# Routed experts of a Perceiver block on sorted tokens: eight expert products of full width become eight passes over nine slots of half-width expert pairs

## What is computed

```python
flat = x.reshape(S, C)                                   # S = 1024 tokens, C = 512
shared = _swiglu(flat @ W_shared_in) @ W_shared_out      # hidden width HID = 1024
g_idx = jnp.argmax(softmax(flat @ Wg_gate + group_bias), -1)      # one of G = 2 groups
in_group = e_group[None, :] == g_idx[:, None]            # 4 of the 8 experts
p_expert = softmax(where(in_group, e_logits, -inf)) * g_prob
topv, topi = jax.lax.top_k(p_expert, 2)                  # w: 2 of 8 weights not zero
h = _swiglu(flat @ W1_shared)
routed = sum over e of  h @ W2_experts[e] * w[:, e:e + 1]
out = _rmsnorm(x + shared + routed, norm2_w)             # and the block adds its input
```

## Time and profile before

| | us |
|---|---|
| median of 3 runs (3694.50 to 3694.57) | 3694.51 |
| profiled execution, its own time | 3685.18 |
| span of that execution | 3683.4 |
| TensorE busy in the span | 3438.0 (93%) |
| dense stage, first matmul at | 3091.47 |
| experts, first matmul at | 3318.20 |

### The profile page before, as it was taken

The page is one execution under the profiler, slowest core; times in us unless marked ns, Lnnn a source line. Parts: engine busy times, 40 slices in busy tenths (PEclk is TensorE's granted clock), DMA queues, the critical chain, the costliest instruction groups (busy, mean ns, idle before and its releaser), DMA issues. The chain is left out here.

```text
span 3683.4 us, 51408 instructions
## 1 busy us (share of the span) xinstructions
PE 3438.0 (93%) x18898; PEld 2918.1 (79%) x18898; DVE 1869.9 (51%) x3079; ACT 1477.5 (40%) x2740; POOL 1583.6 (43%) x1072
## 2 busy tenths in 40 slices
PE   6999999999999999999999978899895867999998
PEld 4888888888888888888888857678774655787886
DVE  3455555455555555554555565665665374221115
ACT  3455555555555555555555421533542142120000
POOL 4455555455545545554555440422431351433440
PEclk9999999999999999999999988999997988999999
DMA  5111111011111101110111041000002101111111
GB/s 206 58 44 42 37 34 43 35 44 44 42 37 44 44 29 39 44 44 35 44 44 36 3 144 35 26 26 1 3 1 89 32 1 43 58 46 46 46 46 40
DMA packets 103901, 161.40 MB, mean 44 GB/s; under 512 B 10192, under 2 KB 70736, under 8 KB 94928
## 3 DMA queue, kind: packets, MB, share of 16 engines
q1 hardware_dynamic: 103632, 158.02, 13.1%
HBM read 139.12 MB, written 18.87 MB: 43 GB/s over the span
## 5 line engine op out<-in xcount | busy, mean ns | idle before, releaser
L427 POOL TENSOR_TENSOR es<-es,e 128x512 f32<-128x512 f32 x480 | 622.2, 1296 | 966.4 <-ACT e L493 966.1
L489 ACT ACTIVATE e_hl<-sc 128x512 fp32r<-128x512 f32 x512 | 323.8, 632 | 738.8 <-DVE sc L557 738.5
L585 PE MATMUL ps_p<-c_hi,wkv_lo 128*128 128x512 f32 x1024 | 402.7, 393 | 4.6 <-PEq L115 4.6
L585 PE MATMUL ps_p<-c_lo,wkv_hi 128*128 128x512 f32 x1024 | 402.4, 393 | 0.0
L585 PE MATMUL ps_p<-wkv_lo,c_hi 128*128 128x512 f32 x1024 | 401.6, 392 | 0.0
L585 PE MATMUL ps_p<-wkv_hi,c_lo 128*128 128x512 f32 x1024 | 401.5, 392 | 0.0
L585 PE MATMUL ps_p<-c_hi,wkv_hi 128*128 128x512 f32 x1024 | 399.3, 390 | 0.0
L515 DVE TENSOR_TENSOR k_lo<-ps_p,k_hi 128x512 fp32r<-128x512 f32 x256 | 175.9, 687 | 440.0 <-ACT k_hi L455 440.0
L585 PE MATMUL ps_p<-wkv_hi,c_hi 128*128 128x512 f32 x1024 | 398.3, 389 | 0.0
L515 DVE TENSOR_TENSOR v_hl<-ps_p,v_hl 128x512 fp32r<-128x512 f32 x256 | 177.3, 692 | 428.1 <-ACT v_hl L455 427.1
L557 DVE TENSOR_SCALAR sc<-ps_s,topi 128x512 f32<-128x512 f32 x512 | 379.9, 742 | 0.3 <-PE ps_s L635 0.2
(11 more groups left out here) (351 smaller groups left out, 7111.1 us busy)
## 6 DMA issues: line engine op xcount, KB each, us to landing
raw<-in_ctx_t SPq DMA_DIRECT2D x64, 1024.0 KB, 4.8
dense_raw<-in_L_ffn_W_experts SPq DMA_DIRECT2D x32, 512.0 KB, 3.6
raw<-in_L_xattn_Wkv SPq DMA_DIRECT2D x4, 1024.0 KB, 4.9
q_hi_scratch<-qa_qh SPq DMA_DIRECT2D x16, 256.0 KB, 2.5
q_lo_scratch<-qa_ql SPq DMA_DIRECT2D x16, 256.0 KB, 3.4
q_hi<-q_hi_scratch SPq DMA_DIRECT2D x32, 128.0 KB, 5.0
q_lo<-q_lo_scratch SPq DMA_DIRECT2D x32, 128.0 KB, 4.7
o_t_scratch<-o_sb SPq DMA_DIRECT2D x32, 128.0 KB, 2.3
```

The lines of the kernel that those rows point to most:

```text
L427: g.tensor_tensor(ES[:, GL], ES[:, GL], e, ALU.add).then_inc(summed, 1)
L489: a.activation(E2[:, s % 2, :, 0, :], sc, ACT.Exp, scale=DH ** -0.5).then_inc(exp_hi, 1)
L585: mm = t.matmul(ps_p[:, par % 2, :], lhs, rhs, start=m == 0, stop=m == 3 * KC - 1)
```

## The change

What it does, in the dense stage:

- Tokens are sorted by group. TensorE counts ranks with 9 small matmuls (`rank`), VectorE makes each token's new place (`place`) and, for each block of 128 sorted tokens, a register value that says which group its first token is of (`steer`, `REGS`). GpSimd scatters rows to three DRAM buffers with indirect DMAs: 8 of the weights and the token's number (`ms_d`), 8 of the rows (`xs_d`), and, after the shared expert, 8 of the sums (`bs_d`).
- The shared expert still runs on the tokens in their old order. Between its output blocks TensorE transposes the sorted rows (`XS`, 8 x 4 transposes), and the second branch runs on sorted tokens.
- The experts: a pass `u` of 8 takes experts p and 4 + p, and of both the same 256 of the 512 output columns (`UNITS`). A block of sorted tokens needs the one half or the other of the 512 columns in SBUF. TensorE loads the block's register (`value_load`) and the 24 matmuls take 256 moving columns from the address made of it. The block in which the groups meet is done twice, for group 0 and (slot `B`, from a copy `HB_hi`, `HB_lo`) for group 1: nine slots in a pass.
- The weights come in the same 4 pieces of 128 x 1,024 for each pass, now as two DMAs of runs of 256 columns.
- The norm is taken after the last slot, four blocks together; GpSimd adds the input rows (8 indirect gathers after the second group of experts) and scatters the result to `out` (8 indirect DMAs).
- Loops over experts are written out.

The diff, cut to the parts that the text speaks of:

```diff
+        HB_hi, HB_lo = (flat(XT_lo[:])[:, n * HK * P:(n + 1) * HK * P].rearrange("p (k f) -> p k f", k=HK) for n in range(2))
...
+        XS = SG
+        X2 = flat(XT_hi[:]).bitcast(F32).rearrange("p (b f) -> p b f", b=B)
+        OUT = ROWS
...
+        NS = B + 1
+        SLOTS = (0, 1, 2, 3, B, 4, 5, 6, 7)
+        UNITS = [(p, o) for p in range(EPG) for o in range(2)]
...
+            def expert_group(u):
+                p, o = UNITS[u]
+                for q in range(GP):
+                    sp.wait_ge(w_lo_done, GP * (u + 4) + q + 1)
+                    dst = RAW[:, q].rearrange("p (k g f) -> p k g f", k=2, g=GROUPS_E)
+                    for g in range(GROUPS_E):
+                        src = w2[EPG * g + p].rearrange("(k p) n -> p k n", p=P)
+                        sp.dma_start(dst[:, :, g, :], src[:, 2 * q:2 * q + 2, o * EH:(o + 1) * EH]).then_inc(raw_in[q], 16)
+
+            def load_sorted(j):
+                sp.dma_start(XS[:, j % 2], xs_d[j * P:(j + 1) * P]).then_inc(xs_in[j % 2], 16)
+            sp.dma_start(ORDER[:], order).then_inc(order_in, 16)
...
+            sp.wait_ge(meta_sent, 16 * B)
+            sp.dma_start(META_S[:], ms_d.rearrange("(b p) f -> p b f", p=P)).then_inc(meta_in, 16)
+            sp.wait_ge(x_sent, 16 * B)
+            sp.wait_ge(h_done, TH * HK)
+            load_sorted(0)
+            load_sorted(1)
+            for j in range(2, B):
+                sp.wait_ge(xs_turned, j - 1)
+                load_sorted(j)
             hidden_group(w1, 3, 0)
+            sp.wait_ge(base_sent, 16 * B)
+            sp.dma_start(ROWS[:], bs_d.rearrange("(b p) f -> p b f", p=P)).then_inc(base_in, 16)
             hidden_group(w1, 4, GP)
-            with sp.Fori(0, E_ALL) as e:
-                out_group(w2[bass.ds(e, 1)].rearrange("o k n -> (o k) n"), e + 5)
-            for b in range(B):
-                sp.wait_ge(final, b + 1)
-                sp.dma_start(out[b], OUT[:, b % 2]).then_inc(stored[b % 2], 16)
-                if b + 2 < B:
-                    sp.dma_start(X2[:, b % 2], x2_d[b + 2]).then_inc(x2_in[b % 2], 16)
-            for par in range(2):
-                sp.wait_ge(stored[par], 16 * B // 2)
+            for u in range(len(UNITS)):
+                expert_group(u)
...
+            def scatter(dst, src, b, sent):
+                g.indirect_dma_start(dst, bass.IndirectOffsetOnAxis(ap=POS[:, b:b + 1], axis=0), src, None).then_inc(sent, 16)
+            g.wait_ge(placed, 1)
+            g.wait_ge(meta_set, 2)
+            for b in range(B):
+                scatter(ms_d, META[:, b], b, meta_sent)
+                scatter(xs_d, ROWS[:, b], b, x_sent)
...
+            g.wait_ge(xs_in[1], 16 * (B // 2))
+            for b in range(B):
+                g.wait_ge(added, b + 1)
+                scatter(bs_d, ROWS[:, b], b, base_sent)
+            split(4, A_)
+            for u in range(len(UNITS)):
+                split(5 + u, (B_, A_)[u % 2])
+                if u == 1:
+                    g.wait_ge(ids_set, 1)
+                    for j in range(B):
+                        g.indirect_dma_start(X2[:, j], None, x2_d.rearrange("b p f -> (b p) f"),
+                                             bass.IndirectOffsetOnAxis(ap=IDS[:, j:j + 1], axis=0)).then_inc(x2_in, 16)
+            g.wait_ge(x2_in, 16 * B)
+            for j in range(B):
+                g.wait_ge(scaled, j + 1)
+                g.tensor_tensor(OUT[:, j], ROWS[:, j], X2[:, j], ALU.add).then_inc(final, 1)
+                g.wait_ge(final, j + 1)
+                g.indirect_dma_start(out.rearrange("b p f -> (b p) f"), bass.IndirectOffsetOnAxis(ap=IDS[:, j:j + 1], axis=0), OUT[:, j], None
+                                     ).then_inc(stored, 16)
+            g.wait_ge(stored, 16 * B)
...
+            a.wait_ge(steered, 1)
+            edge = a.value_load(REGS[0:1, B:B + 1], min_val=0, max_val=B - 1)
+            a.wait_ge(h_hi, 2 * TH * HK)
+            a.copy(HB_hi.rearrange("p k (o f) -> p k o f", o=1), HT_hi[:].rearrange("p k (t f) -> p k t f", f=P)[:, :, bass.ds(edge, 1), :]
+                   ).then_inc(hb_done, 1)
...
+                rank = bank(4)[:, 0:B]
+                link(v.tensor_scalar(N0[:], bank(4)[:, B:B + 1], -1.0, float(TOK), ALU.mult, ALU.add))
+                link(v.tensor_tensor(PA[:], TOKEN, rank, ALU.subtract))
+                link(v.tensor_tensor(PB[:], rank, PA[:], ALU.subtract))
+                link(v.scalar_tensor_tensor(out=PB[:], in0=PB[:], scalar=N0[:], in1=SEL[:, 0, :], op0=ALU.add, op1=ALU.mult))
+                link(v.tensor_tensor(PA[:], PA[:], PB[:], ALU.add))
+                v.tensor_copy(POS[:], PA[:]).then_inc(placed, 1)
...
+                link(v.tensor_scalar(SIDE[:], EDGE, N0[:], None, ALU.is_ge))
+                link(v.tensor_tensor(EDGES[:], SIDE[:, 1:], SIDE[:, 0:B], ALU.subtract))
+                link(v.tensor_copy(REGS[:, 0:B], SIDE[:, 0:B]))
+                link(v.tensor_reduce(PB[:, 0:1], SIDE[:, 0:B], AX.X, ALU.add))
+                link(v.tensor_scalar(PB[:, 0:1], PB[:, 0:1], -1.0, B - 1.0, ALU.mult, ALU.add))
+                link(v.tensor_scalar(PB[:, 0:1], PB[:, 0:1], 0.0, None, ALU.max))
+                v.tensor_copy(REGS[:, B:], PB[:, 0:1]).then_inc(steered, 1)
...
+            for u, (p, o) in enumerate(UNITS):
+                cols = slice(o * EH, (o + 1) * EH)
+                for n, j in enumerate(SLOTS):
+                    m = NS * u + n
+                    v.wait_ge(out_done, B + m + 1)
+                    v.wait_ge(added, B + m)
+                    acc = ROWS[:, j, cols] if j < B else ROWS[:, bass.ds(edge, 1), cols].rearrange("p o f -> p (o f)")
+                    v.scalar_tensor_tensor(out=acc, in0=bank(4 + m % 4)[:, 0:EH], scalar=WS[:, j, p:p + 1], in1=acc,
-                    if last:
-                        v.wait_ge(added, B * u + b + 1)
-                        c.link(rms_scale(v, c, ROWS[:, b], ROWS[:, b], N2[:], stats[:], col[:]))
-                        v.wait_ge(x2_in[b % 2], 16 * (b // 2 + 1))
-                        if b >= 2:
-                            v.wait_ge(stored[b % 2], 16 * (b // 2))
-                        v.tensor_tensor(OUT[:, b % 2], ROWS[:, b], X2[:, b % 2], ALU.add).then_inc(final, 1)
-
-            def weights_of(i):
-                v.wait_ge(added, B * (2 * i + 1))
-                v.tensor_copy(W8i[:], W8[:, :, bass.ds(2 * i, 2)]).then_inc(w8i_done, 1)
-                v.wait_ge(w8i_done, i + 1)
-            c = Chain(v, vchain, 0, 0)
-            v.wait_ge(n2_in, 16)
-            with v.Fori(0, E_ALL // 2 - 1) as i:
-                weights_of(i)
-                expert(i, 0, False)
-                expert(i, 1, False)
-            i = E_ALL // 2 - 1
-            weights_of(i)
-            expert(i, 0, False)
-            expert(i, 1, True)
+            v.wait_ge(added, B + NS * len(UNITS))
+            for hb in range(2):
+                js = range(hb * H_, (hb + 1) * H_)
+                for j in js:
+                    moments(v, c, mom[:, j], ROWS[:, j], stats[:], rs[:, 3, 0:1])
+                s_ = slice(hb * H_, (hb + 1) * H_)
+                link(v.tensor_tensor(rs[:, 0], mom[:, s_, 0], mom[:, s_, 0], ALU.mult))
+                link(v.tensor_tensor(rs[:, 0], rs[:, 0], mom[:, s_, 1], ALU.add))
+                link(v.tensor_scalar(rs[:, 0], rs[:, 0], RMS_EPS, None, ALU.add))
+                rsqrt_cols(v, c, rs[:, 1], rs[:, 0], rs[:, 2])
+                for j in js:
+                    v.scalar_tensor_tensor(out=ROWS[:, j], in0=ROWS[:, j], scalar=rs[:, 1, j % H_:j % H_ + 1], in1=N2[:], op0=ALU.mult, op1=ALU.mult
+                                           ).then_inc(scaled, 1)
+            def rank():
+
+                t_.wait_ge(order_in, 16)
+                t_.wait_ge(ones_set, 1)
...
-            def unit(u, G, r):
-
-                t_.wait_ge(w_lo_done, GP * (G + 1))
-                for b in range(B):
-                    if b >= 4 or not isinstance(u, int) or u > 0:
-                        t_.wait_ge(added, B * u + b - 3)
-                    m = 0
-                    for k in range(HK):
-                        for h, w in ((HT_lo, W_hi), (HT_hi, W_lo), (HT_hi, W_hi)):
-                            mm = t_.matmul(bank(4 + b % 4), h[:, k, b * P:(b + 1) * P], w[:, r, k // 2, (k % 2) * D:(k % 2 + 1) * D],
-                                           start=m == 0, stop=m == 3 * HK - 1)
-                            m += 1
-                    mm.then_inc(out_done, 1)
...
+                for j in range(2 * b, min(2 * b + 2, B)):
+                    t_.wait_ge(xs_in[j % 2], 16 * (j // 2 + 1))
+                    if j >= 2:
+                        t_.wait_ge(xs_lo, j - 1)
+                    for k in range(KC):
+                        mm = t_.transpose(bank(j % 2)[:, k * P:(k + 1) * P], XS[:, j % 2, k * P:(k + 1) * P], I)
+                    mm.then_inc(xs_turned, 1)
...
-            with t_.Fori(0, E_ALL // 2) as i:
-                unit(2 * i + 1, 2 * i + 5, B_)
```

(93 more changed lines are left out.)

139 lines of the change are left out of this document (87 added, 52 removed).

## The result

The changed kernel takes 3588.6 us, median of 4 runs (3586.8 to 3591.4); the kernel before, beside it, 3694.5 us (3692.7 to 3694.6). The ratio is 0.9715, 95% interval 0.9698 to 0.9732: 105.9 us less, where 120.4 were forecast. The profiled execution took 3591.36 us.

What follows compares the result with a forecast made beforehand. TensorE alone was taken to bound the kernel: 1.0 + 207.4 + 31.8 = 240.2 us replace 365.2, earlier parts add 4.6, so 3694.5 - 120.4 = 3574 us; range of 8 in 10: 3560 to 3660.

Steps and rivals of the forecast that it cites:

- forecast A: Experts: TensorE's array paces them, 3574 us, own range 3562 to 3586; chance 0.47.
- Experts, 207.4: Experts on TensorE: 1,728 matmuls of 256 columns at 0.120 us each take 207.4 us, if nothing else paces TensorE.
- The register load, 1.0 bare, and 2.6 us of sequencer in a slot: Expert slots: sequencer work of 2.6 us hides under the array's 2.88; only the first load is bare, +1.0 us.
- rival B: Experts: TensorE's sequencer paces, with gaps in slots that load; 3614 us at 3.5 us a slot, 3658 at 4.2; chance 0.31.
- A register address on a matmul, 0: Expert matmuls: taking the address from a register was priced at nothing, out of 0 to 1.2 us a slot.
- GpSimd's indirect DMAs, 1.2 us: Dense stage: each indirect DMA costs GpSimd 1.2 us, between 0.65 and 2.7; the first 16 fit before the second branch.
- Rival C: GpSimd's indirect DMAs take 2.7 us each, delaying the first splits, the gathers and the end; 3609 us; chance 0.11.
- Earlier parts: Ahead of the experts: `rank` adds 1.1 us and the 32 transposes 3.5, together +4.6 us.
- The branches, forecast at their old length: The two branches of 384 matmuls before the experts were to keep their 88.71 and 87.05 us.
- The end, 31.8: After the last matmul: norm on VectorE, additions and stores on GpSimd, and a landing of 2.3 take 31.8 us.
- The prediction's own sign of a wrong end term: End of the span: GpSimd's last store later than 32 us after the last matmul would show the end mispriced.
- Rival D: Experts: register loads don't run ahead, gaps of 2 us in 64 places; 3740 us at the load's upper price; chance 0.07.

Runs made afterwards that it cites:

- static: Changed kernel without TensorE's register load, the side constant (0 for slots 0 to 3, 1 for 4 to 7); output differs; experts 207.0 us, ratio 0.9693 to the kernel before.
- load2: Changed kernel with each slot's side read into a register twice on TensorE; experts 229.6 us against 208.5, ratio 0.9769 to the kernel before.
- before_shift: Kernel before plus 288 bytes of padding behind W8, giving later buffers the changed kernel's addresses; 3699.9 us against 3695.0, ratio 1.0016.
- pad768: Changed kernel with SEL taking 256 bytes in place of 32, so META and SEL take 768; 3586.5 us, ratio 0.9708 to the kernel before.
- tail_pad: Changed kernel with each row's moments behind its last addition, edge slot first in the last pass, and SEL at 256 bytes; ratio 0.9658 to the kernel before.
- tail_dve: tail_pad with the final x2 additions moved from GpSimd to VectorE and the norm's chain run twice; ratio 0.966 to the kernel before.
- the second profile: The changed kernel run and profiled once more with no edit; ratio 0.971 to the kernel before, dense stage 484.5 us.

## Why the prediction was right, and where it was short

The mechanism of forecast A was right: TensorE's array paces the experts, and 3588.6 lies in 3560 to 3660. The time is 14.5 us over the 3574 given, and 2.6 us beyond A's own range of 3562 to 3586, so the terms around the experts were priced too low. From the first dense matmul 471.5 us were forecast (591.9 - 120.4) and 484.8 came; these 13.3 us are, term by term:

- *Experts, 207.4.* 208.5. The step was right; 1.1 us are the first matmuls behind the pause, at the lower clock (static: 207.0).
- *The register load, 1.0 bare, and 2.6 us of sequencer in a slot.* 0.98 bare; 2.65 to 2.67 us a slot by the first slot and load2. The load was over-priced (0.30 + 0.15 + 0.02 us with its two followers and their gaps are 0.66, not 1.1), the 48 instructions with their register operations under-priced (2.0, not 1.5), and the sum came out right because the two errors cancel, which is luck. The lead put at 17 matmuls, from one operation, holds: of the 56 operations of the earlier trace rows, 52 start when 7 of a block's 24 matmuls have started, 17 ahead of the next block; in the changed kernel 55 of the 64 loads start 17 ahead of their slot's first matmul, 7 of them 16 ahead, and the second one, in the stretch at the lower clock, 12. So rival B was 0.2 us a slot away; load2 crosses the line, and the gap "in each of the eight slots with a load" is what it shows, save for those that the ninth slot covers.
- *A register address on a matmul, 0.* 0 on the array, by static; whether it adds to the sequencer's 2.0 us, no run separates.
- *Weight loads, hidden.* 1,728 pairs of weight load and matmul in 208.5 us are 0.1206 us each: the loads lie beside the matmuls, as the step of 0.120 us in the earlier trace rows had it.
- *GpSimd's indirect DMAs, 1.2 us.* 0.96 and 0.30 of issue, 1.26. `place` was done 17.0 us behind the first matmul (16.5 forecast), the 16 scatters ended at 3142.0, and the second turn waited for no split. Rival C fell by its price.
- *Earlier parts.* Transposes 4 x 0.87 = 3.5, as forecast. `rank` 1.9 (3117.49 to 3119.39) in place of 1.1: 0.8 missed.
- *The branches, forecast at their old length.* 2.6 and 2.6 us missed (the first took 93.2 us, `rank`'s 1.9 among them). This is the step that failed outright: the diff's META and SEL were read for what they hold, and not for what they push. before_shift shows the cost in the old kernel and pad768 gives it back.
- *The end, 31.8.* 38.8, 7.0 missed. The first scaled row was at +8.7, as forecast. The fifth came at +22.4 and not +19.1: VectorE and GpSimd held each other up. The last store was issued by +33.3. Behind it the forecast had 2.3 us of landing, from a store of SP's; it was 5.5, of which GpSimd's closing takes 3.3. The prediction's own sign of a wrong end term, a last store later than 32 us behind the last matmul, is there: it starts at +32.3.
- `rank`'s 0.8, the branches' 5.2, the experts' 1.1 and the end's 7.0 make 14.1; the output blocks and the pauses between the pieces were 0.8 us shorter.

The rest, about a microsecond, lies ahead of the dense stage, where executions differ by more than that. The way in which the forecast was moved to the median (9.3 us over the profiled execution) was sound: the 14 profiles show the early first matmul of the old one (3091.47) to be one end of a spread of 20 us.

Rival D, loads that don't run ahead, fell: in 208.5 us there is no pause behind the first load.

Of the versions, tail_pad has the best ratio, 0.9658 (0.9636 to 0.968), with tail_dve at its side: some 18 us better than the changed kernel in the dense stage (466.5 against 484.8), by a norm that starts before the last matmul and 224 bytes of padding.

## What to carry to other kernels

When a change adds or resizes a buffer, look at what is allocated behind it: the time of matmuls that the diff doesn't touch can move by 3% (0.2267 to 0.2333 us here), and padding is a cheap test. Compare two kernels stage by stage from the stage's first instruction; a span of 3.6 ms hides 5 us that are plain in one stage. In a tail where VectorE and GpSimd take turns on the same rows, price each operation with the other engine's running beside it (1.75 us in place of 0.75 here), and let what can be finished before the last matmul be finished there.

## What the runs showed of the hardware

- The branches' matmuls of 512 columns with weights of their own step at 0.2267 us (256, 768 or 1,024 bytes in META and SEL between the buffers of the two operands; what else lies between them is a multiple of 256) or at 0.2333 us (544, 576, 640). The ninth slot's matmuls of 256 columns, whose operands lie the other way round, step at 0.120 us with 768 or 1,024 bytes and at 0.114 to 0.119 with 544, 576 and 640.
- A register load from SBUF on TensorE takes 0.30 us (median of 64), 0.66 with what follows it, and runs ahead of the array, most often by 17 matmuls: 64 of them cost nothing but the first, 0.98 us.
- A matmul whose address comes from a register costs the array nothing: 420 of them in 50 us with it, and 420 without (static).
- An indirect DMA of 128 rows keeps GpSimd for 0.96 us and 0.30 of issue, up to 2.4 us while VectorE adds rows in SBUF. In the 12 kernels whose last DMA is GpSimd's, its queue's DRAIN takes 3.33 us at the end of the span; in the two whose last DMA is SP's, SP's DRAIN there takes 7 ns.
- After 3.6 us without work, TensorE's first 5 us of experts run at a mean granted clock of 0.66 (they step at 0.12 us at first and behind 3346.65 us, and at 0.21 between), in the second profile at 0.50 (at 0.21 throughout); after 2.6 us, in the one kernel that has it (static), at 1.00.
- On one chip all four kernels of the changed program that were profiled there lost 6 us at the same place, some 4 in a trickle whose cause stays open and some 2 at the lower clock behind it.
